# A hardware loop in place of three written-out passes of an attention stage

## The reference, cut to what matters

```
q  = ln(fp8_linear(ln(x), wq));   k = ln(fp8_linear(ln(x), wk));   v = fp8_linear(ln(x), wv)
core = softmax(q k^T / sqrt(128)) v              # 16 heads, 8 key groups, own 112 tokens
qx = ln(fp8_linear(ln(x), wqx));  kx, vx = split(ctx w_kv_x^T);    kx = ln(kx)
xout = softmax(qx kx^T / sqrt(128)) vx           # the 375 rows of context
x  = x + tanh(g) * fp8_linear(concat(core, xout) / smooth, wproj)
x  = x + tanh(g2) * mixture_of_experts(layernorm(x))       # 8 experts, 2 per token
```

## Time and profile before

| | |
|---|---|
| median of 3 runs | 1268.78 us (1267.77 to 1269.18) |
| profiled execution | 1267.77 us |
| its span, first to last instruction | 1265.6 us |
| PE busy | 1115.5 us, 88% |
| DVE, ACT, POOL busy | 846.6, 706.2, 465.9 us |
| mean granted clock of PE | 0.951 |

### The profile page before, as it was taken

One profiled execution on the slowest core, in us unless ns is written; L12 is line 12 of the kernel. 1 busy time (PEld: TensorE's weight loads), 2 busy tenths in 40 slices (PEclk: granted clock), 3 DMA queues, 4 the chain that ended last, 5 costly groups with the idle time before them and its releaser, 6 DMA issues. The chain is left out here.

```text
span 1265.6 us, 19420 instructions
## 1 busy us (share of the span) xinstructions
PE 1115.5 (88%) x5656; PEld 902.8 (71%) x5656; DVE 846.6 (67%) x1704; ACT 706.2 (56%) x1794; POOL 465.9 (37%) x584
## 2 busy tenths in 40 slices
PE   1089999899999979999988999998799939999996
PEld 1078777678777757877766887876688737777785
DVE  7968877786788778887778777766444665756100
ACT  7966787654776845668765566563122413443442
POOL 3074334244444325433434344441000132556432
PEclk8599999999999989999999999998899959999999
DMA  5041111114111112411111311110546066766220
GB/s 192 17 174 49 33 32 49 41 41 165 40 49 41 33 32 62 160 40 33 47 42 41 124 40 49 41 33 15 174 142 241 18 237 195 206 189 186 53 42 1
DMA packets 51712, 107.37 MB, mean 85 GB/s; under 512 B 5984, under 2 KB 26464, under 8 KB 49568
## 3 DMA queue, kind: packets, MB, share of 16 engines
q1 hardware_dynamic: 46912, 97.00, 23.4%
q0 software_dynamic: 4704, 9.18, 3.3%
HBM read 91.48 MB, written 16.52 MB: 85 GB/s over the span
## 5 line engine op out<-in xcount | busy, mean ns | idle before, releaser
L806 PE MATMUL p_proj<-w_hi,xqs 128*128 128x512 f32 (+2 forms) x464 | 157.9, 360 | 49.1 <-DVE w_lo L529 41.0
L604 POOL TENSOR_TENSOR c_lo<-c_raw,c_hi 128x500 fp32r<-128x500 f32 x96 | 123.9, 1291 | 193.7 <-ACT c_hi L655 193.7
L833 PE MATMUL p_proj<-w_hi,c_hi 128*125 128x512 f32 x384 | 168.7, 439 | 0.0
L591 POOL TENSOR_TENSOR va<-ss,epst 125x2 f32<-125x2 f32 (+1 forms) x180 | 67.3, 374 | 263.3 <-DVE ss L1000 263.1
L833 PE MATMUL p_proj<-w_lo,c_hi 128*125 128x512 f32 x384 | 154.1, 401 | 0.0
L833 PE MATMUL p_proj<-w_hi,c_lo 128*125 128x512 f32 x384 | 153.4, 399 | 0.0
L598 POOL TENSOR_TENSOR rs<-va,mhalf 125x2 f32<-125x2 f32 (+1 forms) x180 | 143.2, 795 | 14.2 <-POOL va L591 0.2
L806 PE MATMUL p_proj<-w_lo,xqs 128*128 128x512 f32 (+2 forms) x464 | 148.1, 339 | 0.0
L1000 DVE TENSOR_REDUCE ss<-sq 125x2 f32<-125x256 f32 (+1 forms) x180 | 89.6, 498 | 83.7 <-ACT sq L665 82.2
L806 PEld LDWEIGHTS p_proj<-w_hi,xqs 128*128 128x128 f32 (+1 forms) x464 | 86.4, 186 | 63.5 <-issue 43.6
L726 ACT ACTIVATE pcross<-p_cross,nmax 112x375 f32<-112x375 f32 x128 | 73.1, 573 | 75.0 <-DVE nmax L1029 71.8
(11 more groups left out here) (234 smaller groups left out, 2732.1 us busy)
## 6 DMA issues: line engine op xcount, KB each, us to landing
c_raw<-in_ctxT SPq DMA_DIRECT2D x96, 250.0 KB, 2.6
shared<-in_w_in SPq DMA_DIRECT2D x16, 1024.0 KB, 9.0
shared<-in_wproj SPq DMA_DIRECT2D x32, 256.0 KB, 3.0
raw_g<-in_Wg SPq DMA_DIRECT2D x8, 1024.0 KB, 6.5
raw_u<-in_Wu SPq DMA_DIRECT2D x8, 1024.0 KB, 7.1
raw_d<-in_Wd SPq DMA_DIRECT2D x8, 1024.0 KB, 5.6
cat_scratch<-cat SPq DMA_DIRECT2D x32, 224.0 KB, 2.0
shared<-cat_scratch SPq DMA_DIRECT2D x2, 1792.0 KB, 8.2
```

The lines of the kernel that those rows point to most:

```text
L591: pool.tensor_tensor(va[0:rows, lo:hi], ss[0:rows, lo:hi], epst[0:rows, lo:hi], ALU.add).then_inc(va_done, 1)
L604: pool.tensor_tensor(flat(c_lo[:, k, :, :]), flat(c_raw[:, k, :, :]), flat(c_hi[:, k, :, :]).bitcast(F32), ALU.subtract).then_inc(cl_done, 1)
L806: m = pe.matmul(out, xqs[:, n, k, 0:rows], (w_hi, w_lo)[i % 2][:, k, lo:lo + w], start=(i == 0), stop=(i == 2 * KB - 1))
L833: m = pe.matmul(bank[0:CT, :], a[:, ch, k, :], w[:, k, CKX:CV], start=(i == 0), stop=(i == 3 * KB - 1))
```

## The change

`passes` makes the loop over the first three passes with `eng.Fori` instead of Python's `range`. The body is then in each engine's program once, and the engine runs it three times, with the number of the pass in a register. What follows from that number (the values of the waits, and the slice of `smi` in `smooth_of`) is worked out by register instructions. The first step (`step(FIRST, ...)`), the rest of the last pass and SP's code stand as before.

```
@@ -515,7 +515,7 @@
         step(FIRST, None, 0, "first", None)
-        for gp in range(GP - 1):
+        with eng.Fori(0, GP - 1) as gp:
             for u in range(1, B):
                 k = u - 2 if 2 <= u < 2 + KB else None
                 step((gp, u), (gp, u - 1), gp + 1, {TJ - 1: "queries", B - 1: "keys"}.get(u), k)
```

## The result

The changed kernel took 1279.34 us (median of four runs, 1277.56 to 1281.84) beside 1268.51 of the kernel before (four runs, 1267.77 to 1269.18): a ratio of 1.0087, 95% interval 1.0068 to 1.0105, or 10.8 us more where 5.0 were forecast, and outside the forecast's own range (1271.4 to 1278). The profiled execution took 1275.52 us with a span of 1273.8.

What follows compares the result with a forecast made beforehand. PE sets the plain steps, a chain through DVE, ACT and PE the other two. Branches 2.2, PE waits 1.7 and ACT waits 1.1 make 5.0 us; with 1.0 from profiled run to median, 1273.8 us, own range 1271.4 to 1278 (chance 0.50).

Steps and rivals of the forecast that it cites:

- The sign: Whole kernel: slower by over 0.2%, chance 0.72; within 0.2% 0.24, faster 0.04.
- DVE's stall: After cat behind a taken branch: 3.0 us of fetch delays the second sums by 1.0, hidden beside PE's 1.1 us lateness.
- PE's gap at the branch: Before p_proj opens a pass: 3.0 us fetch less 1.9 us lead shows 1.1 us, at two branches 2.2 us.
- The 0.2 us for two branches with nothing fetched: Loop's two taken branches: at about 108 ns each without fetching, the sum would be 3.0 us instead of 5.0.
- The moved waits: Waits now taken by a register or wait instruction ahead of the work: 0.06 us each, 1.7 us on PE, 1.1 on ACT.
- PE's 28: PE's moved waits at p_out (15), turned nkx (3) and turned pcross (10): 0.06 us each, 1.7 us.
- ACT's 75: ACT's exponentials waiting for DVE's maxima: 4.5 us at 0.06 each, only the quarter in chain-set steps counted, 1.1 us.
- One: Branches and moved waits: nothing shows, code arrives within PE's lead or is still held; 1269.5 us, chance 0.24.
- Two: Branch back: DVE's code waits 6 us behind SP's 4 MB of weights, PE idles and its clock falls; 1282 us, chance 0.13.
- Three: DVE's chain-set steps: 72 added register instructions show at 0.06 us in three passes, 13 us; 1284 us, chance 0.09.
- Four: Gap at nkx (3.74 us) stays short, saving a clock fall of 1.1 us a pass, 3.3 in three; 1265.5 us, chance 0.04.

Runs made afterwards that it cites:

- hints: Changed kernel with a branch prefetch hint at the loop's head on all four engines, registers and moved waits kept; 1273.87 us, ratio 1.0027 to the kernel before.
- POOL's wait: Kernel before, with POOL's second split of the context waiting until DVE has scaled nq; 1262.02 us, ratio 0.9952. Also added to other kernels.

## Why the prediction was wrong

The sign, the places and the branch's mechanism were right; the size was off by more than double, through the term for DVE's stall, the terms for the waits, and one that was missing.

**PE's gap at the branch** stood. Forecast 1.1 us twice: from the start of p_out's first row (L898) to that of p_proj, 1.36 and 1.35 us before, 2.33 and 2.79 after, so 0.97 and 1.44, put down to issue, and none at the third place. In part it was luck: the fetch was taken as 3.0 us and took 3.41 and 3.88, and the lead that hides it was taken as 1.9 and was 2.44 both times (3.41 - 0.97, 3.88 - 1.44). The 0.2 us for two branches with nothing fetched, which the prediction set beside its own term, is ruled out, while POOL's branch is as free as that reading had it.

**DVE's stall** was to hide: "everything that it waits for comes 1.1 us later anyway". As far as nmax, on which ACT waits, it does: nmax starts 4.91 and 5.41 us behind cat's start, 3.94 and 3.93 before, so 0.97 and 1.48 later, PE's gap to 0.04 us. But the first sums, which before had run as soon as cat was done, stand behind the stall too, and POOL's rstd of them with its second split. The changed kernel at the first branch:

```profile
299.69 1.49 DVE L1000 TENSOR_REDUCE ss<-sq 128x4 f32<-128x512 f32 x2 [2.80 <-issue]
...
300.81 1.01 POOL L598 TENSOR_TENSOR rs<-va,mhalf 128x4 f32<-128x4 f32 x1 [0.16 <-POOL va L591]
301.09 0.61 DVE L1015 TENSOR_REDUCE nmax<-p_self 112x4 f32<-112x448 f32 x1
301.79 1.26 POOL L604 TENSOR_TENSOR c_lo<-c_raw,c_hi 128x500 fp32r<-128x500 f32 x1
301.86 1.75 DVE L1009 TENSOR_TENSOR nq<-nq,rs 128x512 f32<-128x512 f32 x1
```

The scale of nq waits there for nearly the whole split, 1.75 us for 1.21 before. Those 0.5 us, with 0.5 of registers in that step, fill up (1,0): 2.2 for 1.1. At the second branch the scale took 1.26, and registers and PE's gap make the 2.0. Forecast for both branches 2.2, measured 4.24, of which 1.05 are registers (1.05 with hints, 1.09 without a branch), so 3.2 against 2.2.

**The moved waits** are, by the medians, the step that failed most: 2.8 us of the sum, and registers without any branch cost 7.0 (1.0055), though only 2.7 of them in the loop of the profile. They were put on the wrong engine. PE's 28 (1.7 us) cost nothing that shows, so it did not hold either that what is added to PE's stream in a plain step is paid in full. ACT's 75 were counted at a quarter, "in plain steps PE's surplus covers them". It does not: registers on ACT alone lengthen plain steps by 0.10 us at 0.13 a wait, for 2.5 us in all (forecast 1.1) with POOL's wait, 6.6 without.

By places the two profiles of the changed kernel have 4.3 and 4.6 us in the steps behind the branches (forecast 2.2), 5.0 and 2.0 in the steps (x,6) and (x,7) (forecast 2.8, in these), and 1.0 and 0.7 in the other plain steps (forecast 0).

**The port was missing** from the list of parts. It also explains why plain steps in the changed kernel looked mixed: POOL's later split gives back 0.1 to 0.2 us, and in steps (1,3) and (1,4) the scale of nqx takes longer. Kernel before, then the changed one, in step (0,3):

```profile
173.42 1.25 POOL L604 TENSOR_TENSOR c_lo<-c_raw,c_hi 128x500 fp32r<-128x500 f32 x1 [2.53 <-ACT c_hi L655]
174.19 1.02 DVE L1009 TENSOR_TENSOR nqx<-nqx,rs 128x512 f32<-128x512 f32 x1
```

```profile
174.08 1.26 POOL L604 TENSOR_TENSOR c_lo<-c_raw,c_hi 128x500 fp32r<-128x500 f32 x1 [2.75 <-ACT c_hi L655]
174.66 1.23 DVE L1009 TENSOR_TENSOR nqx<-nqx,rs 128x512 f32<-128x512 f32 x1
```

The scale starts 0.58 us behind the split where it was 0.77, so it waits 0.21 us longer. It is the same in all of them: of the plain steps not behind a branch, in both profiles of the changed kernel and in the one with hints, those with a scale of 1.22 us or more, and no others, grew by 0.23 to 0.31 us.

**The clock.** After its wait for pcrossT the changed kernel's second pass shows a half clock that the kernel before hasn't (windows of 2 us, first the changed kernel, then before):

```profile
474.78 1.11 PE L898 MATMUL p_out<-pselfT,val 112*128 112x224 f32 x2 [1.99 <-DVE pcrossT L1047]
...
474.00:476.00 2.00, 1.22 (x3) 1.16 (x4) 0.97 (x3) 0.00 (x0) 0.87 (x2) 0.50 0.00 0
476.00:478.00 2.00, 2.00 (x7) 1.78 (x7) 0.00 (x0) 0.00 (x0) 0.02 (x1) 0.50 0.00 0
```

```profile
470.15 0.65 PE L898 MATMUL p_out<-pselfT,val 112*128 112x224 f32 x2 [1.92 <-DVE pcrossT L1047]
...
470.00:472.00 2.00, 1.85 (x9) 1.81 (x10) 0.45 (x3) 0.00 (x0) 0.89 (x2) 1.00 0.00 0
```

The step (1,6) is 2.1 us longer with it, and 0.44 in the second profile of the changed kernel, which lacks it (clock 1.00 there), so it costs 1.7: such a fall comes with some executions. Another moves: with the loop on ACT alone, and with its registers alone, it stands at 280 us, in (0,7), where the kernel before has it at 254, in (0,6). First before, then the loop on ACT alone:

```profile
252.00:256.00 4.00, 3.32 (x15) 2.29 (x15) 2.58 (x8) 3.40 (x9) 1.31 (x2) 0.74 0.02 1
...
278.00:282.00 4.00, 3.89 (x20) 2.87 (x19) 3.97 (x8) 2.01 (x7) 2.50 (x3) 1.00 0.08 8
```

```profile
252.00:256.00 4.00, 1.92 (x11) 1.25 (x11) 3.47 (x10) 4.00 (x13) 0.68 (x1) 1.00 0.00 0
...
278.00:282.00 4.00, 2.72 (x13) 2.00 (x14) 3.78 (x12) 3.06 (x9) 1.34 (x2) 0.81 0.18 57
```

That is where the 1.50 us of its steps (x,7) lie, in each pass. With POOL's wait they are gone. What chooses the place of a fall stays open, and with it how much of the median's 10.8 us is falls: the second profile of the changed kernel has 7.3 us in the loop and 5.8 outside it, and 27 runs of the kernel before on one chip lay between 1264.77 and 1277.69 us.

**The rivals.** None was it. One had nothing show, and 10.8 us did. Two had a dear branch behind the 4 MB of weights: both branches have that load right behind them (issued at 297.55 and 509.75 us), and DVE stood 2.8 and 2.6 us, not 6. Three had register work dear on DVE: 0.3 us in the profile, 3.3 at the median. Four had the gap at nkx shorter: it is 3.88 us in the first pass, for 3.74.

## What to carry to other kernels

At a far branch back DVE and ACT went 2.4 to 3.1 us and PE 3.4 to 3.9 us without code (bodies of 557 to 2035 instructions), POOL with its 215 nearly none, and what such a stall delays is all work queued behind it and whoever waits for that, not only the next wait; a prefetch hint at the head took it away here. A wait that a register instruction takes made ACT's next operation 0.13 us later in a chain that set the steps, and PE's 0.07 us later without longer steps. Before pricing a change in tenths of microseconds, look for operations of DVE and POOL that take twice their shortest time: such a meeting can turn over by 0.08 us, and a wait that settles it was worth more (6.6 us) than the change itself was feared to cost.

## What the runs showed of the hardware

- Who takes the port is not to be read from the starts of rows. In the kernel before and in the one with the loop on POOL alone the split's row starts 0.58 and 0.50 us ahead of the scale's, yet in the one DVE waits and in the other POOL.
- It isn't only two-input operations: DVE's scaling of pcross, one tile and a column of factors, waited too (1.21 for 0.42 us), while its casts of bf16 and its maxima out of PSUM kept their times beside the split. There the split took as much longer (2.33 us for 1.25) as the three casts took (1.09), so it may be the casts that it waited for; no run tests it.
- The pass number in a register, which gives PE 215 register steps a pass, cost 0.9 us at the median, within the interval of none (1.0007, 0.9991 to 1.0023).
- The loop made the chip fetch more code, not less: 120 packets for 96.
